# Graph network on one core, edge count: two constant 128x512 products ahead of each group of 56 tiles, and the weights' loads on ScalarE's queue

## The reference, cut to what matters

```python
z = concat([h[src], h[dst], edge_attr])                 # layer 0: gated convolution
agg = segment_sum(sigmoid(bn(z @ W_int + b)) * softplus(bn(z @ W_upd + b)), dst)
summed = segment_sum(h[src], dst)                       # layer 1: mean over neighbours
vals = mask * d_inv_sqrt[row] * d_inv_sqrt[col]         # layer 2: three hops with learned masks
x = segment_sum(vals[:, None] * x[col], row)
msg = relu(concat([h[src], edge_attr]) @ W1 + b1) @ W2 + b2   # layer 3: edge MLP, mean, layer norm
```

## Time and profile before

| what | us |
|---|---|
| runs, median of 3 | 11239.33 (11235.35 to 11245.48) |
| span of the profiled execution | 11234.0 |
| TensorE matmul busy, share of the span | 8366.9 (74%) |
| VectorE busy | 8649.2 (77%) |
| ScalarE busy | 6257.6 (56%) |
| GpSimd busy | 5047.9 (45%) |

### The profile page before, as it was taken

The page is one execution under the profiler, slowest core; times in us unless marked ns, Lnnn a source line. Parts: engine busy times, 40 slices in busy tenths (PEclk is TensorE's granted clock), DMA queues, the critical chain, the costliest instruction groups (busy, mean ns, idle before and its releaser), DMA issues. The chain is left out here.

```text
span 11234.0 us, 448798 instructions
## 1 busy us (share of the span) xinstructions
PE 8366.9 (74%) x151748; PEld 7090.9 (63%) x151749; DVE 8649.2 (77%) x21890; ACT 6257.6 (56%) x14808; POOL 5047.9 (45%) x5196
## 2 busy tenths in 40 slices
PE   6444444378889997996877788778887788777877
PEld 6444344278877777886756667467675576655855
DVE  6776667578889999998686785976868858679367
ACT  0222222169987777997405536975359863589410
POOL 1777777734430001111371471753726627356057
PEclk8555555589999998998999989999889998899999
DMA  6655553269989997996996998979989789897997
GB/s 220 185 179 183 180 168 90 70 215 330 331 281 259 258 248 261 322 322 210 329 328 247 290 271 301 312 248 288 272 285 316 242 302 272 274 322 256 373 326 264
DMA packets 1297726, 2929.45 MB, mean 261 GB/s; under 512 B 381368, under 2 KB 925682, under 8 KB 1272400
## 3 DMA queue, kind: packets, MB, share of 16 engines
q1 hardware_dynamic: 956540, 1976.18, 51.0%
q0 software_dynamic: 296704, 823.09, 24.7%
q10 hardware_dynamic: 44116, 125.96, 4.0%
HBM read 1753.54 MB, written 1104.99 MB: 254 GB/s over the span
## 5 line engine op out<-in xcount | busy, mean ns | idle before, releaser
L574 POOL DMA_INDIRECT rows_s<-place_rec,place_index x1568 | 1523.3, 971 | 531.0 <-issue 514.2
L665 PE MATMUL place_slot_ps<-place_runs,place_oh_turned 50*128 50x100 f32 x3136 | 728.5, 423 | 1072.5 <-ACT place_oh_turned L613 1025.6
L2959 POOL DMA_INDIRECT hop_x<-cols_all,hop_index x864 | 988.3, 1144 | 1024.1 <-ACT hop_index L2968 757.5
L665 PEld LDWEIGHTS place_slot_ps<-place_runs,place_oh_turned 50*128 50x128 f32 x3136 | 683.1, 327 | 1103.3 <-issue 1091.3
L2977 ACT ACTIVATE hop_parts<-hop_x,mask 128x64 f32<-128x64 f32 x5184 | 1258.7, 336 | 10.7 <-issue 6.6
L3024 PEld LDWEIGHTS hop_sums_ps<-hop_parts,hop_onehot 128*128 128x128 bf16 x18144 | 587.4, 97 | 650.6 <-issue 649.9
L1853 POOL DMA_DIRECT2D cm_onehot<-hot_d x288 | 152.7, 531 | 1774.4 <-POOLq L107 977.8
L3024 PE MATMUL hop_sums_ps<-hop_parts,hop_onehot 128*128 128x64 bf16 x18144 | 687.7, 193 | 334.2 <-DVE hop_parts L3006 321.5
L2764 POOL DMA_INDIRECT mask_cols<-cols_all,mask_index x432 | 432.6, 1001 | 790.9 <-ACT mask_index L2788 679.6
L2761 POOL DMA_INDIRECT mask_cols<-cols_all,mask_index x432 | 672.1, 1556 | 254.0 <-ACT mask_index L2788 162.7
L622 ACT COPY place_rec<-keys 128x32 f32 (+1 forms) x98 | 21.5, 219 | 1309.7 <-DMA place_rec<-in_e 1261.1
(11 more groups left out here) (498 smaller groups left out, 28533.6 us busy)
## 6 DMA issues: line engine op xcount, KB each, us to landing
cols_all<-att_in_rows SPq DMA_DIRECT2D x216, 896.0 KB
mask_onehot<-hot_s SPq DMA_DIRECT2D x108, 1792.0 KB
cols_all<-hop_in_rows SPq DMA_DIRECT2D x216, 896.0 KB
hop_onehot<-hot_s SPq DMA_DIRECT2D x864, 224.0 KB
rows_all<-blank SPq DMA_DIRECT2D x72, 1808.0 KB
ct_u<-rows_all SPq DMA_DIRECT2D x288, 452.0 KB
cm_v<-rows_all SPq DMA_DIRECT2D x288, 448.0 KB
cm_onehot<-hot_d POOLq DMA_DIRECT2D x288, 448.0 KB
```

The source lines that it names most:

```text
L574: nc.gpsimd.indirect_dma_start(m.rows_s.rearrange("p n w -> (p n) w"), bass.IndirectOffsetOnAxis(index[:, j, t:t + 1], 0), rec[:, j, t, :] ...
L665: last = nc.tensor.matmul(slot_ps[b][:, t, 0:2 * NBK], oh_turned[:, b, t, :], runs[:, b, t, :], start=True, stop=True)
L2959: nc.gpsimd.indirect_dma_start(x[:, n, :, :].rearrange("p c f -> p (c f)"), None, table, bass.IndirectOffsetOnAxis(index[:, n:n + 1], 0)). ...
```

## The change

It does two things in `stage_count`. At the head of `add_up`, before the wait for the group's one-hots, TensorE issues two products of the identity with 512 columns of `numbers_wide` into a bank of PSUM of their own, which nobody reads. And the 60 loads of weights move from SyncE's queue, where they stood behind the clearing of `rows_s`, to ScalarE's, where they stand ahead of the three DMAs of the table; ScalarE waits for them at the stage's end. The loads wait for `made` to reach 1, the clearing of `w_att2` by GpSimd that one of them would otherwise overwrite too early.

```diff
@@ stage_count
+        warm = ps("warm_ps")
+        numbers_flat = m.numbers_wide[:].rearrange("p n t -> p (n t)")
...
             def _(sp):
-                loads = weight_loads(m, a)
                 sp.wait_ge(made, 4)
                 for g in range(NBS // ROWS):
                     sp.dma_start(m.rows_s[:, g * ROWS * C:(g + 1) * ROWS * C, :], empty[:]).then_inc(cleared, 16)
-                for to, of in loads:
-                    sp.dma_start(to, of, allow_slow_non_contiguous=True).then_inc(loaded, 16)
-                sp.wait_ge(loaded, 16 * len(loads))
                 sp.wait_ge(cleared, 16 * (NBS // ROWS))
...
             def _(act):
+                loads = weight_loads(m, a)
+                act.wait_ge(made, 1)
+                for to, of in loads:
+                    act.dma_start(to, of, allow_slow_non_contiguous=True).then_inc(loaded, 16)
                 act.wait_ge(tabled, 1)
                 act.dma_start(flat_dram.rearrange("a (p q) -> p a q", q=QR), table_i[:]).then_inc(flat, 16)
...
                 act.wait_ge(flat, 48)
+                act.wait_ge(loaded, 16 * len(loads))
...
                 def add_up(b, j, first, last):
+                    for c in range(2):
+                        nc.tensor.matmul(warm[:], m.ident_b[:], numbers_flat[:, c * 512:(c + 1) * 512], start=True, stop=True)
                     pe.wait_ge(hot, b + 1)
```

## The result

| | before | with the change |
|---|---|---|
| median, us (6 runs each) | 11240.15 (11228.1 to 11245.5) | 11267.33 (11257.0 to 11290.7) |
| span of the profiled execution, us | 11234.0 | 11266.0 |
| ratio | | 1.0028, 95% interval 1.0018 to 1.0039 |
| counts read by VectorE at, us | 184.27 | 214.19 |
| next stage's first matmul at, us | 196.51 | 226.33 |

Slower, as forecast, but by more: +23.4 us were predicted and the stage itself is 29.8 us longer, 0.27% of the span. The median of 11267.3 lies within the range of 11249 to 11271; the ratio on the median of before gives 11240.15 x 1.0028 = 11271.6, just above its top.

The account below looks back on a forecast made before the run. TensorE was taken to bound the count at 1.2 GHz; 23.1 for products + 0.5 for changing weights - 0.2 at the end = +23.4 us, so 11239.3 + 23.4 = 11262.7 us, range 11249 to 11271.

Parts of the forecast that it names:

- What bounds the stage: In the count, TensorE was said to be the bound at 5.33 us a group, VectorE having 2.27 us to spare.
- how many pairs count: Of 28 pairs in the count the first is free, 27 cost 0.854 us each: 23.1 us.
- what the loads cost: Loads on ScalarE's queue cost 0, issued by 193 us before the table is due; rival of late loads 0.02.
- Which clock the count had: The count was said to run at 1.2 GHz, though the window column reads 1.00.
- The neighbour of rows 9: Eight contiguous 128x50 matmuls at 0.50, 0.08 us each, taken as agreeing with the count's 95 ns at 1.2 GHz.
- Whether the pair lifts the clock: In the count the clock stays down, as 0.85 us of unbroken streaming over all rows per group is not enough; chance 0.83.
- Part 1, the products: Two products of 512 columns per group at 1.2 GHz, 0.427 us each, 0.854 us together.
- Part 3, changing weights: Loading the identity and returning to the one-hots costs 0.02 us per group, 0.5 us in all (0 to 2.6).
- The end: At the count's end VectorE no longer comes after TensorE: -0.2 us.
- The rival of a raised clock: In the count the clock rises and stays up, matmuls down to 47.5 ns: -59 us, 11180; chance 0.09.
- The sentence on the cachelines: Skill note that accesses crossing to a new line each time pay a penalty; by it the clock gives less than half back.
- The second rival: Clock already up in the count, or rising without speeding its reads: products 0.216 us each, +11.7 us, 11251; chance 0.06.

Follow-up runs that it names:

- e1: The change without the pair of products, only the loads moved to ScalarE's queue: ratio 1.0000 (0.9990 to 1.0009).
- e2: The change with the pair of products but the loads left on SyncE's queue: ratio 1.0030 (1.0018 to 1.0041).
- e7: The change with 40 products of 512 columns at the stage's start and no pair per group: period 5.32 us, counts read at 184.49 us.
- e9: The change without the pair, plus a probe of six kinds of matmul on constants after the last group: both operands packed 44 ns at 0.50, strided 95.
- e6: The change, pair kept, with 40 more products of 512 columns at the stage's start: ratio 1.0014 (1.0004 to 1.0024).
- e3: The change with one product of 512 columns per group instead of two: period 6.02 us, one run at 11251.9 us.
- e8: The change with six products per group instead of two: period 8.13 us in the mean, 11297 us.
- e16: The change without the pair, one-hots laid out for operands strided by 2 elements, VectorE's constant packed 50x2: ratio 0.9945, 11180.65 us.
- e4: The change with the two products taking 50 columns of weights instead of 128: period 6.16 us, one run at 11234.9 us.
- e13: The change without the pair, one-hots laid out for operands strided by 2 elements, VectorE's constant still strided by 112: ratio 0.9999 (0.9991 to 1.0008).
- e10: Probe on constants after the last group, 50x50 matmuls at strides of 2 to 112 elements and VectorE comparisons: stride 2 took 45 ns, 8 took 94.

## Why the prediction was right or wrong

- *What bounds the stage; how many pairs count; what the loads cost.* Right: TensorE with 27 of 28 pairs on the path, the loads 0 (e1, e2), issued by 129.6 where I allowed 193.
- *Which clock the count had.* Right, and now recorded: 0.50 with the count's exact period in e7. The 1.00 of rows 5 was an empty entry; the first record in the trace of before is a rise at 203.6 us. One leg of the argument was weak. The neighbour of rows 9 reads both operands packed, and e9's packed matmuls take 44 ns at 0.50, not its 81. So its closeness to the count's 95 ns was chance and no sign of the clock. What holds it isn't shown; in the program its output stands apart in PSUM, nine f32 from column to column, where e9's is packed.
- *Whether the pair lifts the clock.* Right that it does not (e6: 0.50 through all groups; between e3 and the change a product costs 0.427 us). The reason given is half borne out: more products do raise it (e8), but unbroken streaming is not needed (e16).
- *Part 1, the products.* Right: 0.84 us for two in e4, 0.43 between e3's one and the change's two.
- *Part 3, changing weights.* **This step failed.** I took 0.02 us a group, with 0.095 as the upper end, because in a hop 384-column products stand between matmuls with no gap. But there both sides load 128 columns of weights, which costs nothing in e9 either. Here the pair cuts into loads of 50, and that costs 0.27 us a group (e3, e4), 27 x 0.25 = 6.8 us more than the sum had. The bound from above was one step of the count, and nothing in the trace justified it: a row of another mix is no upper end for this one. With 0.27 the sum is 23.1 + 7.3 - 0.2 = 30.2, against 29.8 measured.
- *The end.* The 0.2 us fell away as said: VectorE is ready 2.11 us before the counts.
- *The rival of a raised clock.* Its price of -59 us was wrong for this kernel: it halved the count matmul with the clock, and the matmul does not depend on it (e8, e9). At the full clock the pair would still have cost 27 x 0.43 or more. The sentence on the cachelines had named the reason, but the forecast set it against the 81 ns of rows 9 and so left most of the 95 ns to the clock. The stage was worth nearly those 59 us all the same, by another way (55.6 in e16). The second rival, a clock that was up already, is out by e7's record. Its 0.216 us for 512 columns is 0.213 by the row it was taken from; e9 has 0.216.
- *Chances.* The 0.56 stood for slower by over 0.2%. The ratio of +0.28% lies above that border, but its interval (0.18 to 0.39%) still touches it; the stage's 29.8 us are 0.27%.

## What to carry to other kernels

Before paying for a higher clock, see whether the matmul that is meant to gain follows the clock at all: its spacing beside its columns at 1.2 GHz (here 95 ns against 50 columns, 42 ns) says that something else holds it, and a burst of the same form on packed constants tells what. One strided operand of the two is enough to hold a matmul, and the repair may move the stride onto another engine's operand, so look at both sides' durations after it (e13). A stride of 8 bytes that looks free at the low clock can still hold the matmul at the high one (e10). A foreign instruction in a stream is priced from a row of the same mix or not at all: the 0.02 us came from a stream of 128-column weights and the true price was over ten times that. And a part that is hidden today (the loads) should be priced again when its cover goes: 0 us before, 16.8 us after.

## What was not expected of the hardware

- 50-column bf16 matmuls, start to start: 44 ns packed, 45 at a stride of 2 elements, 49 at 4, 94 at 8, 87 to 95 beyond. At the full clock the packed ones and those with a stride of 2 take 26 ns, a stride of 4 still 49, and strides of 8 and 112 the same 94 and 95 (e9, e10, e16).
- A stream of strided 50-column matmuls left for two 128-column products and taken up again loses 0.27 us per visit; with 50-column weights in the products, or 128-column weights in the stream, nothing (e4, e9).
- The clock column reads 1.00 where there is no record yet. In the profiled execution of the changed kernel no record comes before 2.3 ms, so the whole of the next stage reads 1.00, and the mean clock of the execution 0.956 instead of 0.861, with the transposes as slow as before. Other executions of both kernels show either mean, so it is no property of the change. A mean or a slice of that column says nothing until the first change of the clock is on record.
- A VectorE comparison of bf16 took 3.07 us with its constant packed in pairs and 5.4 us with the same pairs 224 bytes apart.
